# Three edge passes and a linear-attention mix on one core: gathers of 128 rows, node rows added by VectorE in half of the pairs, one-hots built by ScalarE, and GpSimd's sums of the mix moved to VectorE

## The reference

```python
def _gatv2(x, src, dst, eattr, Wl, Wr, We, att, b, n):      # twice in layer 0: passes 1 and 2
    xl, xr, ee = x @ Wl, x @ Wr, eattr @ We
    xj = xl[src]
    h = leaky_relu(xj + xr[dst] + ee, 0.2)
    logits = h @ att
    m = segment_max(logits, dst, n)
    ex = exp(logits - m[dst])
    denom = segment_sum(ex, dst, n)
    return segment_sum(xj * (ex / denom[dst])[:, None], dst, n) + b
# layer 1, eight heads of 32: pass 3
    e = leaky_relu(eh[src] + ee + et[dst], 0.2)             # one number per edge and head
    ex = exp(e - segment_max(e, dst)[dst]); a = ex / segment_sum(ex, dst)[dst]
    rst = segment_sum(ft[src] * a[:, :, None], dst) + bias
# layer 1, the mix ("second mix")
    q, k, v = split(x @ W_qkv + b_qkv, 3); q, k = q - mean(q), k - mean(k)
    k2 = l2_normalize(k*k / (sum(k*k) + 1e-7), axis=nodes)
    q2 = l2_normalize(q*q / (sum(q*q) + 1e-7), axis=features)
    out = (v + q2 @ (k2^T v) / sqrt(N)) @ W_out + b_out
```

## Time and profile before

| | us |
|---|---|
| median of 3 runs | 5197.01 (5194.62 to 5203.74) |
| profiled execution, its own time | 5204.3 |
| its span in the trace | 5202.5 |
| TensorE busy | 4340.8 (83%) |
| VectorE busy | 2738.6 (53%) |
| ScalarE busy | 2171.7 (42%) |
| GpSimd busy | 2022.1 (39%) |
| gathers `msg_rows` in all three passes | 1649.9 (1296 of them) |

### The profile page before, as it was taken

One profiled execution on the slowest core, in us unless ns is written; L12 is line 12 of the kernel. 1 busy time (PEld: TensorE's weight loads), 2 busy tenths in 40 slices (PEclk: granted clock), 3 DMA queues, 4 the chain that ended last, 5 costly groups with the idle time before them and its releaser, 6 DMA issues. The chain is left out here.

```text
span 5202.5 us, 73734 instructions
## 1 busy us (share of the span) xinstructions
PE 4340.8 (83%) x21745; PEld 3584.4 (69%) x21746; DVE 2738.6 (53%) x8592; ACT 2171.7 (42%) x6651; POOL 2022.1 (39%) x1623
## 2 busy tenths in 40 slices
PE   9589999999995899988699998749936888878694
PEld 8478879788794777765577776438935666655694
DVE  2263452634523666764366666363355777766324
ACT  2243434434442666652366666122243333333222
POOL 0000000000004888840488885106618888833141
PEclk9789999999997999996899999659965666579697
DMA  5510000000005555530455553472267656620613
GB/s 141 145 52 10 18 10 1 18 10 18 1 21 124 126 126 125 125 88 19 98 125 127 129 125 83 93 219 68 63 146 151 136 135 135 134 67 25 202 36 87
DMA packets 364626, 463.24 MB, mean 89 GB/s; under 512 B 166429, under 2 KB 296743, under 8 KB 363790
## 3 DMA queue, kind: packets, MB, share of 16 engines
q1 hardware_dynamic: 172546, 258.16, 19.5%
q0 software_dynamic: 191744, 200.92, 17.5%
HBM read 396.61 MB, written 60.67 MB: 88 GB/s over the span
## 5 line engine op out<-in xcount | busy, mean ns | idle before, releaser
L656 POOL DMA_INDIRECT msg_rows<-tab_d,msg_cur x1296 | 1649.9, 1273 | 1762.8 <-DVE msg_cur L142 1368.7
L908 PE MATMUL msg_agp<-msg_rows,msg_oh 125*125 125x261 f32 (+2 forms) x2592 | 849.5, 457 | 14.3 <-DVE ga_acc L792 10.7
L908 PEld LDWEIGHTS msg_agp<-msg_rows,msg_oh 125*125 125x125 f32 x2592 | 549.0, 223 | 125.1 <-DVE ga_acc L792 18.2
L862 PE MATMUL msg_zp<-g_xr,msg_oht 127*125 x1728 | 544.3, 396 | 64.5 <-DVE msg_oht L696 64.2
L866 PE MATMUL msg_zp<-msg_rows,c_ident 125*125 125x256 f32 x1728 | 528.9, 387 | 81.9 <-DMA msg_rows<-tab_d,msg_cur 81.5
L701 DVE SCALAR_TENSOR_TENSOR msg_hid<-msg_zp,g_att 125x256 f32<-125x256 f32 x864 | 360.8, 420 | 334.3 <-PE msg_zp L866 329.5
L960 ACT ACTIVATE msg_dist<-c_iota,c_rel 125x125 f32<-125x125 f32 x1296 | 493.3, 387 | 49.7 <-PEq L3077 34.7
L964 ACT ACTIVATE msg_oh<-msg_dist,c_ones 125x125 f32<-125x125 f32 x1296 | 493.5, 387 | 0.0
L950 ACT ACTIVATE msg_ex<-msg_arg 125x16 f32<-125x16 f32 (+1 forms) x81 | 20.0, 247 | 984.9 <-DVE msg_delta L766 984.9
L866 PEld LDWEIGHTS msg_zp<-msg_rows,c_ident 125*125 125x125 f32 x1728 | 323.9, 190 | 153.7 <-DMA msg_rows<-tab_d,msg_cur 103.6
L792 DVE TENSOR_TENSOR gv_acc<-gv_acc,msg_agp 125x261 f32 (+1 forms) x864 | 364.4, 422 | 72.4 <-PE msg_agp L908 64.9
(11 more groups left out here) (552 smaller groups left out, 7221.1 us busy)
## 6 DMA issues: line engine op xcount, KB each, us to landing
msg_oht<-rel_d SPq DMA_DIRECT2D x81, 875.0 KB
msg_rows<-tab_d,msg_cur POOLq DMA_INDIRECT x1296, 3.9
pl_raw<-in_edge_attr SPq DMA_DIRECT2D x25, 448.0 KB
msg_pens<-pen_d SPq DMA_DIRECT2D x270, 31.2 KB
msg_oht<-rel_d SPq DMA_DIRECT2D x81, 101.6 KB
mix_w<-in_L_mix_W SPq DMA_DIRECT2D x8, 1024.0 KB
m0w_wr<-in_L_ffn_w SPq DMA_DIRECT2D x16, 512.0 KB
m0w_w2r<-in_L_ffn_w SPq DMA_DIRECT2D x16, 512.0 KB
```

Source lines behind the costliest of these rows:

```text
L656: nc.gpsimd.indirect_dma_start(out=rows[:, q, k, :], out_offset=None, in_=table, in_offset=bass.IndirectOffsetOnAxis(ap=cur[:, q, k:k + 1] ...
L862: nc.tensor.matmul(z, hots, d_t, start=True, stop=False)
L908: nc.tensor.matmul(agp[:, sum_bank(u, k), 0:AW], oh[:, u % RB, k, :], rows[:, u % RB, k, 0:AW], start=True, stop=True).then_inc(summed.sem, 1)
```

## The change

Six things change, three in the one-head passes, one in all passes, one in pass 3 and one in the second mix.

1. A gather fetches 128 rows instead of 125: `rows`, `cur` and `src_s` are 128 partitions tall (three of them padding).
2. With one head, the odd pairs of a turn (`by_vector`, four of eight) have no identity products. VectorE adds the pair's rows itself (`add_rows`, one tensor_tensor of 125x512 from PSUM and SBUF into `both`), which also frees the PSUM bank, and takes both relus of the pair from `both` one step later.
3. `node_hots` moves from VectorE to ScalarE, as two activations of 125x2000 ahead of `weights(j)`. `edge_hots` takes 16 activations of 125x125 and 4 of 125x500 instead of 32, works in place in `oh`, and so waits until the group three back has been aggregated.
4. The one-head `rescale` is a tensor_tensor with a broadcast factor instead of a tensor_scalar.
5. With eight heads the scores of group j+1 stand in the first half of the turn, four per pair, and `logits(j+1)` stands at step 10.
6. In the second mix GpSimd's block is gone. VectorE does `sums` in the loop over tiles, `closed` is cut in two, its second half and the shift (`base`) go to the output loop, and the loop is one round shorter.

```diff
+ROWS = 128
...
-        rows = st.sb("rows", [P, RB, G, TW])
-        cur = st.sb("cur", [P, RB, G], I32)
+        rows_all = st.sb("rows", [ROWS, RB, G, TW])
+        rows = rows_all[0:P]
+        cur = st.sb("cur", [ROWS, RB, G], I32)
...
+        def by_vector(p):
+            return p % 2 == 1
...
-                            nc.gpsimd.indirect_dma_start(out=rows[:, q, k, :], out_offset=None, in_=table,
+                            nc.gpsimd.indirect_dma_start(out=rows_all[:, q, k, :], out_offset=None, in_=table,
...
-                def node_hots(g, u, lap):
-                    dve.wait_ge(hots_landed[u % RB].sem, hots_landed[u % RB].at(lap * hots_in + hots_in))
-                    nc.vector.tensor_scalar(oht[0:P, u % RB], oht[0:P, u % RB], c.part[0:P, 0:1], None, ALU.is_equal).then_inc(oht_ready.sem, 1)
+                def add_rows(g, u, p):
+
+                    n = added_pair(g, p)
+                    if n >= 2:
+                        dve.wait_ge(relu_done.sem, relu_done.at(n - 1))
+                    dve.wait_ge(z_ready.sem, z_ready.at(g * PAIRS + p + 1))
+                    z = zp[:, pair_bank(u, p), 0:2 * D].rearrange("p (a f) -> p a f", a=2)
+                    nc.vector.tensor_tensor(both[:, n % 2], z, rows[:, u % RB, 2 * p:2 * p + 2, 0:D], ALU.add).then_inc(z_used.sem, 1)
...
+                    src = both[:, n % 2, k % 2] if by_vector(p) else zp[:, pair_bank(u, p), (k % 2) * D:(k % 2 + 1) * D]
+                    last = nc.vector.scalar_tensor_tensor(out=hid[:, k % 4, :], in0=src, scalar=0.0, in1=att[:],
                                                           op0=ALU.max, op1=ALU.mult, accum_out=lgr[:, u % RB, k:k + 1])
...
-                        ch(nc.vector.tensor_scalar(a_t, a_t, fac[:, u % RB, 0:1], None, ALU.mult))
+                        ch(nc.vector.tensor_tensor(a_t, a_t, fac[:, u % RB, 0:1].broadcast_to([P, W]), ALU.mult))
...
                         if one and not final:
-                            relu(j + 1, u + 1, k)
+                            if not by_vector(k // 2):
+                                relu(j + 1, u + 1, k)
+                            elif k % 2 == 0:
+                                add_rows(j + 1, u + 1, k // 2)
+                            else:
+                                relu(j + 1, u + 1, k - 1)
+                                relu(j + 1, u + 1, k)
...
                         if k == 9 and not final and spare:
-                            node_hots(j + 2, u + 2, i + (u + 2) // RB)
                             take_sources(j + RB, u)
+                        if not one and not final and k == 10:
+                            logits(j + 1, u + 1, i + (u + 1) // RB)
...
-                    if not final:
+                    if one and not final:
                         logits(j + 1, u + 1, i + (u + 1) // RB)
...
-                        last = nc.tensor.matmul(z, c.ident[0:P, 0:P], rows[:, u % RB, k, 0:D], start=False, stop=True)
+                        if not by_vector(k // 2):
+                            last = nc.tensor.matmul(z, c.ident[0:P, 0:P], rows[:, u % RB, k, 0:D], start=False, stop=True)
...
+                        if not final and not one and p < PAIRS // 2:
+                            if p % 2 == 0:
+                                nts = node_tiles(j + 1, p // 2)
+                            for k in range(4 * p, 4 * p + 4):
                                 score(j + 1, u + 1, k, nts[k % (G // 2)], i + (u + 1) // RB)
...
+                    if g >= RB:
+                        act.wait_ge(summed.sem, summed.at((g - RB + 1) * G))
+                    for b in range(5):
+                        if b < 4:
+                            for k in range(b * QS, (b + 1) * QS):
+                                last = nc.scalar.activation(oh[:, u % RB, k, :], c.iota[0:P, 0:P], ACT.Abs, scale=-1.0, bias=c.rel[:, bass.ds(g * G + k, 1)])
+                            last.then_inc(dist_ready.sem, 1)
+                        if b == 0:
                             continue
...
+                        quarter = oh[:, u % RB, (b - 1) * QS:b * QS, :]
+                        last = nc.scalar.activation(quarter, quarter, ACT.Relu, scale=-1.0, bias=c.ones[0:P, 0:1])
...
+                def node_hots(g):
+
+                    act.wait_ge(hots_landed[g % RB].sem, hots_landed[g % RB].at((g // RB + 1) * hots_in))
+                    h = oht[0:P, g % RB]
+                    nc.scalar.activation(h, h, ACT.Abs, scale=-1.0, bias=c.part[0:P, 0:1]).then_inc(far_ready.sem, 1)
+                    act.wait_ge(far_ready.sem, far_ready.at(g + 1))
+                    nc.scalar.activation(h, h, ACT.Relu, scale=-1.0, bias=c.ones[0:P, 0:1]).then_inc(oht_ready.sem, 1)
...
                 def body(j, u, final=False):
+                    if j + 2 < NG:
+                        node_hots(j + 2)
                     weights(j, u)
...
-                    nc.gpsimd.tensor_tensor(ksum[:], ksum[:], kk[:, t % R], ALU.add).then_inc(kk_summed.sem, 1)
...
-                    nc.gpsimd.tensor_tensor(x2[:, t], x2[:, t], shift[:], ALU.add).then_inc(based.sem, 1)
...
-                    nc.gpsimd.tensor_tensor(k2sum[:], k2sum[:], k2[:, t % R], ALU.add).then_inc(k2_summed.sem, 1)
...
+                def sums(t):
...
+                    nc.vector.tensor_tensor(ksum[:], ksum[:], kk[:, t % R], ALU.add).then_inc(kk_summed.sem, 1)
+                    nc.vector.tensor_tensor(k2sum[:], k2sum[:], k2[:, t % R], ALU.add).then_inc(k2_summed.sem, 1)
...
+                def base(t):
+
                     row = x2[:, t].rearrange("p (h f) -> p h f", h=HEADS)
...
+                    nc.vector.tensor_tensor(row, row, acc4[:, t, :, 0:DH], ALU.add).then_inc(closed_ready.sem, 1)
+                    dve.wait_ge(closed_ready.sem, closed_ready.at(NT + t + 1))
+                    nc.vector.tensor_tensor(x2[:, t], x2[:, t], shift[:], ALU.add).then_inc(x2_ready.sem, 1)
```

More of the change, by code:

```diff
@@ L413, in _ @@
                 dve.sem_inc(pens_ready.sem, 1)
-                take(1, c.src_s[:, 0:S], bank[0][0:P, 0:S])
+                take(1, c.src_s[0:P, 0:S], bank[0][0:P, 0:S])
                 take(2, c.last[:], bank[1][0:P, 0:S])
@@ L582, in messages @@
         pens = st.sb("pens", [R, RB, 4, P])
-        hid = st.sb("hid", [P, G, D]) if one else None
+        hid = st.sb("hid", [P, 4, D]) if one else None
+        both = st.sb("both", [P, 2, 2, D]) if one else None
         lgr = st.sb("lgr", [P, RB, G]) if one else None
@@ L831, in _ @@
                     for k in range(G):
+                        if k % 2 == 0 and by_vector(k // 2):
+                            add_rows(0, 0, k // 2)
                         relu(0, 0, k)
@@ L1819, in _ @@
                 ch(nc.vector.reciprocal(zero[:], d))
+                ch(nc.vector.tensor_tensor(shift[:], bq[:, 2], bias[:], ALU.add))
                 def evict(t):
@@ L1863, in _ @@
                 nc.vector.tensor_scalar_mul(kn[:], kn[:], ROOT).then_inc(kn_ready.sem, 1)
-                dve.wait_ge(x2_ready.sem, x2_ready.at(NT))
+                dve.wait_ge(bvo_ready.sem, bvo_ready.at(1))
+                ch(nc.vector.tensor_tensor(shift[:], shift[:], bvo[:], ALU.add))
+                dve.wait_ge(closed_ready.sem, closed_ready.at(NT))
+                for t in range(2):
+                    base(t)
                 for t in range(NT):
+                    if t + 2 < NT:
+                        base(t + 2)
+                    dve.wait_ge(x2_ready.sem, x2_ready.at(t + 1))
                     dve.wait_ge(out_done.sem, out_done.at(t + 1))
```

81 lines of the change are left out of this document (39 added, 42 removed).

## The result

The changed kernel takes 5390.8 us (median of 4 runs, 5379.6 to 5405.9) beside 5195.8 us for the kernel before: a ratio of 1.038 with a 95% interval of 1.034 to 1.042. It is slower, and the prediction, 4965 us in 4885 to 5100, was wrong. The profiled execution has a span of 5390.5 us at a mean clock of 0.826.

What follows compares the result with a forecast made beforehand. Passes 1 and 2 were taken as bound by GpSimd's gathers and TensorE's chain, pass 3 by TensorE and VectorE, the second mix by VectorE. Savings of 173 + 40 + 19 = 232 us gave 4965 us, range 4885 to 5100.

Steps and rivals of the forecast that it cites:

- The gathers: GpSimd's gathers in the edge passes: 128 rows take 1.05 us plus 0.30 between gathers, so 21.6 us per turn.
- The line through two row counts: Gather price from 125 and 108 rows: 12.6 ns per row, negative at zero rows; carried on, upper bound 1.25 us.
- rival C: 128-row gathers no dearer than 108: GpSimd needs 20.8 us per turn, TensorE's chain decides, 4925 us; chance 0.25.
- Turn of passes 1 and 2: GpSimd sets turns of 21.8 us, above 20.9 for the TensorE and VectorE chain; saves 173 us with the fills.
- A: The forecast itself: GpSimd's turn of 21.8 us, between 21.3 and 22.8; total 4940 to 5015 us; chance 0.40.
- VectorE's pairs: Passes 1 and 2: TensorE loses eight identity products, 3.46 us per turn; VectorE takes four additions, 2.7 us.
- eight relus from SBUF: Relus reading SBUF might hold up GpSimd's gathers: turn 3.4 us longer, 25.0; part of a rival with chance 0.20.
- rival D: Passes 1 and 2: TensorE has more gaps, its clock falls to 0.61, turn 32.6 us, about 5513 us; chance 0.04.
- tipping point: Passes 1 and 2: falling clock decides from turns of 26.3 us, with 30% of TensorE's work at the low level.
- Pass 3: Earlier logits save half of the 3.10 us boundary wait: turn 24.4 us from 25.90, 37 us plus 3.
- Second mix: GpSimd's block and a VectorE instruction leave the loop: 0.77 us per tile, 19 us; bounds nothing and 26.
- The sum: Whole kernel: 173 + 40 + 19 = 232 us saved, 4972 us profiled, forecast 4965 us.

Runs made afterwards that it cites:

- a_rows_126: The changed kernel with gathers of 126 rows instead of 128: 4937 us, 0.950 of the kernel before; on another chip 5416 us, 1.034.
- c_before_rows_128: The kernel before with only its gathers changed to 128 rows, on a chip with pauses: 5539 us, 1.058 of the kernel before.
- d_rows_125: The changed kernel with gathers of 125 rows again, on a chip with pauses: 5142 us, 0.980 of the kernel before.
- a_no_vector_pairs: The changed kernel without pairs added by VectorE, all identity products back on TensorE: 5033 us, 0.966 of the kernel before.

## Why the prediction was wrong

**The step that failed** is "The gathers", by "That gives 16 x (1.05 + 0.30) = 21.6 us per turn": it takes GpSimd's busy time as the whole price of a gather. GpSimd's part came out at 0.949 us in the median, and GpSimd was indeed no bound any more. But on the chip of the result, and on B, C, D and E, the results of TensorE's products reach VectorE late while such gathers follow each other every 1.25 to 1.30 us. No row of the kernel before shows that, and I had no rival in which a quicker gather costs another engine something. The rivals all moved the price of GpSimd, or the clock by itself. In pass 1 it is VectorE's 75.1 + 22.6 us of "remote" waits in 24 turns, 4.1 us per turn, and a clock of 0.87, that is some 7 us of each turn at the low level, which lengthen TensorE's work by up to 3.6 us (an estimate). Together that is somewhat more than the 6.3 us between 28.0 and the 21.7 of an undisturbed turn (`a_rows_126`); presumably a part of it lies over waits that stand anyway. The fills add 27 us to pass 1 and 25 us to pass 3. That the pauses come with the wide gathers is shown by runs of one edit (`c_before_rows_128` at 1.058, `d_rows_125` at 0.980). What inside the chip does it is open, and so is why the runs on chip A have none.

**Point by point**, against chip A, where no pause disturbs the sum (the changed kernel itself was not run there; its version with 126 rows stands for it):
- Gather: forecast 1.05 us, measured 0.949 in the median for 128 rows and 0.997 for 126. The line through two row counts was rightly set aside. The Trainium skill, DMA: Bandwidth & Descriptors, section "Why a DMA increments its semaphore by 16 and not by 1", gives 126 rows 14 engines with 9 rows each, the same 9 as 108 rows. The traces agree with it if the price goes by rows per engine: 0.997 us for 126 and 0.999 for 108. With 8 rows it is 0.949 and with 25 it is 1.214, so rival C was right in kind, and its price (0.985, on a straight line) 0.04 too high.
- Turn of passes 1 and 2: forecast 21.8 us, with 20.9 for the chain of TensorE and VectorE. The 24 full turns of `a_rows_126` behind its second rescale take 21.7 us each (1691.2 to 2211.2; the last one, 13.5 us, is short). GpSimd was not the bound there (377 of 533.5 us busy); the chain was, at 0.8 us more than I gave it. So it was rival C's mechanism that held on chip A, and that it gave A's 21.8 is luck: a gather that was too dear stood in for a chain that was too short.
- VectorE's pairs: the difference of `a_no_vector_pairs` and `a_rows_126`, 96 us, is 1.9 us per turn in two passes (the two differ in the rows of a gather too, 128 and 126, but GpSimd is the bound of neither). TensorE lost 3.46 us of products, and 1.6 of them did not come back; that the handoffs took them is likely and not shown. The eight relus from SBUF held no gather up that mattered: the median of `a_rows_126` is 0.997 us.
- The other side, rival D: not the cause, since with the same short TensorE the clock is 1.00 on chip A. The clock fell behind the pauses, not for want of products. Its tipping point was right in kind: at 28 us the total was above that of the kernel before.
- Pass 3: forecast 24.4 us; full turns of 23.9 in `a_rows_126`. So 2.0 of the 3.10 us at the boundary came back, more than the half that I took. With the pauses, in the changed kernel, nothing did (26.1).
- Second mix: forecast 19 us, measured 22 (575.1 to 553.5 us behind pass 3). Its evictions are 3.09 us apart instead of 3.85, so 0.76 us per tile came back of the 0.77 forecast. L1880 takes 0.41 us and L1891 0.42 from first to last:

```profile
L1862 DVE TENSOR_TENSOR sq_qk<-sq_pq,sq_bq x25: 679/682/692, 4868.4 to 4942.5; 125x512 f32<-125x512 f32 x25
...
L1880 DVE TENSOR_SCALAR ga_ee<-sq_sq,sq_rec,sq_qn x25: 411/413/416, 4877.2 to 4948.1; 125x256 f32<-125x256 f32 x25
...
L1891 DVE TENSOR_TENSOR ga_acc<-ga_acc,sq_zero x25: 415/417/421, 4869.1 to 4945.3; 125x256 f32<-125x256 f32 x25
```

- The sum: 4965 us forecast, 4937 us for the 126-row version on chip A. Its terms were within a microsecond per turn, in part because two misses cancelled; what it left out decided the sign.

## What to carry to other kernels

A change that makes transfers come quicker wants a rival in which a third engine pays: here the gather became cheaper for GpSimd (1.273 to 0.986 us), and VectorE paid with its waits for TensorE. When a result contradicts itself between two experiments, run the same programs again on one chip before taking the kernel apart: here two groups of runs were spent on a partner of the gather that did not exist. The version to keep is the change with 125-row gathers, 0.980 and 0.985 of the time before on two chips, and not the 126-row one, which is 0.950 on one and 1.034 on another.
